# Last cross-attention of a two-layer decoder: TensorE does the projections of later pairs ahead of the weighting of the values in each slot

## The reference

```python
x = _layernorm(x, ln_media_w, ln_media_b)          # context, 77 rows
lat = _layernorm(latents, ln_lat_w, ln_lat_b)      # 512 rows
q = lat @ Wq + bq
kv_in = jnp.concatenate([x, lat], axis=1)
kv = kv_in @ Wkv + bkv
k, v = jnp.split(kv, 2, axis=-1)
...
sim = jnp.einsum('bhid,bhjd->bhij', q * scale, k)
attn = jax.nn.softmax(sim, axis=-1)                # less the row's maximum
out = jnp.einsum('bhij,bhjd->bhid', attn, v)
...
return out @ Wout + bout
```

## Time and profile before

| | us |
|---|---|
| median of 3 runs | 1188.86 |
| lowest, highest | 1175.42, 1189.67 |
| the profiled execution, its own time | 1190.02 |
| its span in the trace | 1188.3 |
| PE busy | 1091.5 (92%) |
| PEld busy | 916.1 (77%) |
| DVE busy | 738.3 (62%) |
| ACT busy | 608.6 (51%) |

### The profile page before, as it was taken

The page is one execution under the profiler, slowest core; times in us unless marked ns, Lnnn a source line. Parts: engine busy times, 40 slices in busy tenths (PEclk is TensorE's granted clock), DMA queues, the critical chain, the costliest instruction groups (busy, mean ns, idle before and its releaser), DMA issues.

```text
span 1188.3 us, 18015 instructions
## 1 busy us (share of the span) xinstructions
PE 1091.5 (92%) x6794; PEld 916.1 (77%) x6794; DVE 738.3 (62%) x1733; ACT 608.6 (51%) x1128; POOL 153.0 (13%) x115
## 2 busy tenths in 40 slices
PE   6779999999997468999999999999999999999896
PEld 3558778888886346888889888889888898889532
DVE  5854776556565776666665766665666657663246
ACT  5235543332335436565664656664566656664353
POOL 6110220026625232000000000000000000000001
PEclk9956878999998667999999999999999999999998
DMA  6100000000001000000000000000000000000001
GB/s 221 6 1 1 1 1 1 1 1 1 1 1 36 1 0 1 2 1 2 2 1 2 2 1 2 2 1 2 2 1 2 1 1 2 1 1 2 1 0 36
DMA packets 15680, 10.11 MB, mean 9 GB/s; under 512 B 8759, under 2 KB 14827, under 8 KB 15083
## 3 DMA queue, kind: packets, MB, share of 16 engines
q1 hardware_dynamic: 15595, 8.96, 2.6%
HBM read 7.60 MB, written 1.05 MB: 7 GB/s over the span
## 4 chain that ended last, share of the span: by engine, by line
PE 71%; ACT 15%; DVE 8%; issue 5%; POOL 1%; DMA 0%; POOLq 0%; ACTq 0%; DVEq 0%
PE PS L1399 66%; ACT KA L855 9%; ACT BIG L872 4%; PE PS L1411 4%; PE PS L1761 1%; DVE st L912 1%; DVE X_ODD L923 1%; DVE BIG L1006 0%; DVE mx L1003 0%; DVE X_EVEN L923 0%; DVE mv L915 0%; DVE mxm L1284 0%; ACT BIG L673 0%; ACT BIG L665 0%; DVE VXA L1251 0%
## 5 line engine op out<-in xcount | busy, mean ns | idle before, releaser
L1399 PEld LDWEIGHTS PS<-VXA,BIG 128*128 128x128 f32 (+1 forms) x3136 | 395.9, 191 | 48.1 <-ACT BIG L872 24.5
L1399 PE MATMUL PS<-VXA,BIG 128*128 128x65 f32 (+2 forms) x3136 | 398.4, 272 | 9.4 <-ACT BIG L872 9.4
L872 ACT ACTIVATE BIG<-PS 128x512 f32<-128x512 f32 (+1 forms) x320 | 187.3, 595 | 177.3 <-PE PS L1399 174.4
L1284 DVE TENSOR_REDUCE mxm<-PS 128x1 f32<-128x512 f32 x256 | 170.7, 688 | 96.4 <-PE PS L1399 92.1
L855 ACT ACTIVATE KA<-PS,b1s 64x512 fp32r<-64x512 f32 (+1 forms) x256 | 128.7, 503 | 52.1 <-PE PS L1399 46.4
L1399 PE MATMUL PS<-QA,KA 128*128 128x512 f32 (+1 forms) x320 | 145.1, 453 | 0.0
L548 POOL TENSOR_TENSOR rs<-ve,half_neg 128x4 f32<-128x4 f32 (+1 forms) x29 | 30.1, 1038 | 882.4 <-DVE ve L917 882.4
L1399 PE MATMUL PS<-QB,KB 128*128 128x512 f32 (+1 forms) x320 | 125.6, 393 | 0.0
L1399 PE MATMUL PS<-KA,QA 128*128 128x512 f32 (+1 forms) x512 | 115.8, 329 | 1.8 <-DVE mxm L1284 1.6
L1399 PEld LDWEIGHTS PS<-KA,QA 128*128 128x128 f32 x512 | 86.8, 190 | 21.7 <-DVE mxm L1284 3.6
L777 ACT ACTIVATE BIG<-PS 128x512 f32<-128x512 f32 x72 | 42.7, 599 | 95.7 <-PE PS L1399 95.4
(11 more groups left out here) (249 smaller groups left out, 1584.1 us busy)
## 6 DMA issues: line engine op xcount, KB each, us to landing
X_EVEN<-in_x SPq DMA_DIRECT2D x4, 256.0 KB, 3.9
VXA<-in_L_ffn_Wg SPq DMA_DIRECT2D x1, 1024.0 KB, 5.7
VXA<-in_L_ffn_Wu SPq DMA_DIRECT2D x1, 1024.0 KB, 7.8
VXA<-in_L_ffn_Wd SPq DMA_DIRECT2D x1, 1024.0 KB, 9.5
REG<-in_L_xattn_Wkv SPq DMA_DIRECT2D x1, 1024.0 KB, 4.8
QB<-crow SPq DMA_DIRECT2D x64, 2.0 KB
out<-X_EVEN SPq DMA_DIRECT2D x4, 256.0 KB, 2.3
wq1s<-in_L_xattn_Wq SPq DMA_DIRECT2D x1, 512.0 KB, 8.4
```

Of the source, the lines that this page charges most:

```text
L872: act.activation(PX[0:rows, g % 4, :], PS[0:rows, g % 2, :], ACT.Exp, scale=SCALE_W).then_inc(pw_ready, 1)
L1284: dve.tensor_reduce(mxm[:, p % 2, h, m:m + 1], PS[:, 2 + g % 2, :], AX.X, ALU.max).then_inc(mu_free, 1)
L1399: return pe.matmul(dst, lhsT, rhs, start=start, stop=stop, **kw)
```

## The change

In each slot, the tasks other than "oT" and "yE" now stand ahead of the weighting `pv` in TensorE's order. "oT" and "yE" stay behind it. The tables and the orders of ScalarE, VectorE, GpSimd and SyncE are the same.

```diff
                     if p + 1 < PAIRS:
                         for u in MAX_UNITS.get(slot, []):
                             max_unit(p + 1, u)
+                    for key in tasks.get(slot, []):
+                        if key[0] not in ("oT", "yE"):
+                            task(key)
                     if SLOTS * p + slot:
                         pv(SLOTS * p + slot - 1)
                     for key in tasks.get(slot, []):
-                        task(key)
+                        if key[0] in ("oT", "yE"):
+                            task(key)
```

## The result

The changed kernel takes 1237.01 us (median of 4 runs, 1234.91 to 1241.71) against 1189.26 us before (4 runs beside it, 1175.42 to 1199.72). The ratio is 1.046, 95% interval 1.0394 to 1.0527: slower by 48 us. The forecast was 1208 with a range to 1217. The new wait and its price came as forecast; a fall of TensorE's clock, which makes more than half of the loss, did not. Executions of one kernel fall into a faster and a slower group: medians here are of all of them, ratios and intervals compare the faster ones alone.

A forecast was written before the change was run, and what follows sets the result against it. TensorE's own work was taken to bound the last cross-attention stage, with about 10 us of holes. Per pair +1.23 for c's stall and -0.60 for slot 7's wait, over 30 pairs +18.9 us: 1208 us, range 1198 to 1217.

The forecast's parts named there:

- The new wait and its price: Slot 6: TensorE stalls 1.17 us at transpose c for K's PSUM bank; slot 7's QB comes 1.23 us later a pair.
- Slot 7's wait goes: Slot 7: K and Kt are evacuated earlier, so the wait for slot 6's exponential disappears, -0.60 us a pair.
- pv(4) later by Kt's 0.34, chain of 1.48 us to c: Slots 5 to 6: Kt delays pv(4) 0.34 us; VectorE's reciprocal to c's load takes 1.48 us, so c starts at 943.96.
- From c to slot 7's QB 1.24 us: Slot 6: after c, pv(5) starts from a standing engine; slot 7's QB follows 1.24 us later, at 945.20.
- Weight loads pulled ahead: Slot 6: pv(5)'s first load done during c's wait would save 0.11 us a pair, 3.3 in all; not assumed.
- Q, V and K in slots 0, 2 and 3 free: Slots 0, 2, 3: products ahead of weightings cost nothing; K's bank is free with 0.14 to 0.19 us to spare.
- V in slot 7 free: Slot 7, 15 pairs: Kt's bank is freed by 944.6, V is reached at 945.2, so no cost.
- Sum of the costed terms +18.9 us: Whole stage: 1.23 - 0.60 = +0.63 us a pair over 30 pairs, +18.9 us.
- rival D: TensorE's clock falls to 1.2 GHz in 3 pairs of the stage: +24 us on top, 1232 us; 4%.
- Rival C: K in slot 3 misses Q's bank, or the delayed odd head holds up score matmuls: +5 to +11, 1213 to 1219 us; 19%.
- A: Only the gain: c's wait is covered and slot 7's wait goes, -18 us, 1171 us; 7%.
- B: No net change: gain and c's stall about equal, or ScalarE the pair's true clock, 1186 to 1201 us; 8%.

The follow-up runs named there:

- e2: The kernel before with c alone moved ahead of the weighting: 1222.06 us, ratio 1.020 to the kernel before.
- e4: The changed kernel with VectorE doing `lo` of K's second half ahead of the even head's reciprocal and division in slot 5: 1176.77 us, 0.982 of the kernel before.
- e1: The changed kernel with c put back behind the weighting, Q, K, Kt and V staying ahead: 1183.35 us, 0.988 of the kernel before.
- e5_pad2: The changed kernel with two more 512-column matmuls in slot 6 of every pair, ahead of the scores: 1215.43 us, 1.023 of the kernel before.
- e10_lo_twice: The kernel before, TensorE's order untouched, with VectorE doing `lo` of K's second half twice: 1202.43 us, 1.001 of the kernel before.

## Why the prediction was right or wrong

- *Slot 7's wait goes, -0.60 a pair*: right, 0.58 in the mean. 1.35 us from QB to QB, no wait on L872 left; e2, e4 and e1 show the same.
- *pv(4) later by Kt's 0.34, chain of 1.48 us to c*: right. c came 1.40 us behind slot 6's QB, as the forecast's 943.96 - 942.56; the chain took 926.67 - 925.18 = 1.49. The wait row of c's load shows 1.44 us and that of its matmul 1.01, where I had named 1.1 to 1.3 for the load.
- *From c to slot 7's QB 1.24 us*: 1.30. c's own load (926.67 to 926.74) stands in front of pv(5)'s. I had put nothing on it and named 0.11 as the bound. +0.06 x 30 = 2 us.
- *Weight loads pulled ahead*: pv(5)'s load starts 0.07 us behind c's, not before it. Nothing is pulled past the load that stands; the full price was right. The row that I had argued from was no evidence: there c's load came as the loads in front of it ended (942.67 + 0.97), and hardly waited.
- *Q, V and K in slots 0, 2 and 3 free*: right, no matmul wait ahead of any of them. *V in slot 7 free*: true in the changed kernel only because c's stall covers it; e1 shows 0.34 us of load wait in 15 pairs once the stall is short.
- *Sum of the costed terms +18.9 us*: 19.8 measured by e5_pad2. Had the clock held, the changed kernel would have taken about 1210 us.
- *The clock, put at nothing in the sum and 4% as rival D*: this is the step that failed. The sum took the stage at full clock; eight falls, 61 us at half clock, cost about 29 us, past the 24 of rival D. The mechanism was named and then dismissed with two readings that do not bear it. I set the new stall of 1.2 us against "the 0.75 us load waits of every pair" that the clock had stood; but those are waits of loads, of which the matmul row had 0.32 us. Like for like, the change made TensorE's regular standing time three times what this stage had shown to be harmless. And I argued from the one row ahead of the stage with TensorE half idle, which is no bound for a case in between. A row for nearly this length did exist, in an earlier stage of the kernel before (waits of the matmul row; then its stretch):

```profile
...
PE PS L1411 <- DVE X_ODD L923: 1.8, 2, 0.9
...
205.00:375.00 170.00, 166.00 (x1001) 142.89 (x999) 101.48 (x269) 60.04 (x124) 71.01 (x11) 1.00 0.02 7
...
```

  Two gaps of 0.9 us passed there at full clock. They would have been no clearance either, for 22 of the changed kernel's 30 stalls passed too: two gaps that pass say little about 30. The trace of before had no row for a regular stall over 0.32 us, and so none for the 4%; e10_lo_twice shows falls from 0.62 us of it.
- *Rival C, a second bank wait, 19%*: did not come in the changed kernel. *A and B*: refuted by 30 waits of 1.01 us.

What stays open: what tells the eight stalls from the 22 that pass, why e2_c_only with 0.67 us had eight falls, e10_lo_twice with 0.62 us three and e5_pad2 with 0.54 us none. One profile of each does not tell chance from rule.

## What to carry to other kernels

When an operation is moved earlier on a full engine, ask not only what it delays but whether its own operands are ready there: here c had a slack of 0.06 us, and the weighting taken from in front of it had been its cover. An instruction that waits exactly as long as the work in front of it is a chain already; shorten the chain first (VectorE's two operations exchanged), then move. And price a new stall on TensorE twice: as lost time, and for what it may do to the clock. Hold it against matmul gaps, not load waits, and against gaps that come as regularly: single long ones at full clock do not clear it.

## What the runs showed of the hardware

A stall of TensorE of 1.0 us in each of 30 pairs, about 21 us apart, in a stage in which its matmul row was still busy 661 of 692 us, went with eight falls of the granted clock to 1.2 GHz; a stall of 0.62 us, put into a stage that had none, went with three, and stalls of 0.54 us (e5_pad2) and 0.31 us (before) with none, each by one profiled execution. Each fall lasted 3.4 to 10.2 us. The eight of them, 61 us long, cost about 29 us: QB matmuls stood 2.56 us apart instead of 1.35. The gaps filled with matmuls whose result is thrown away, the same kernel was 20 us faster. A weight load that waited 1.44 us held back the next one, which started 0.07 us behind it.
